# Decoder layer, one core: the FFN's weights are rounded and turned inside eleven attention rounds and kept in DRAM, and the preparation stage between the two parts is taken out

## What is computed

```python
x = x + attention(layernorm(x))                  # 16 heads of 32, causal, q k v o weights 512x512
x = x + long_conv_mixer(ctx, ctx, layernorm(x))  # head_dim 8, 32 heads, filters of length 512
x = x + ffn(layernorm(x))

def _quant_dequant(v, axis):                     # one scale for each row
    scale = jnp.maximum(jnp.max(jnp.abs(v), axis=axis, keepdims=True) / QMAX, EPS)
    return jnp.clip(jnp.round(v / scale), -QMAX, QMAX) * scale
# ffn, I = 1408
xq  = _ste(x, axis=-1);  w1q = _ste(w_gate_up, axis=-1)      # w_gate_up: 2816 x 512
gate_up = einsum('bsh,oh->bso', xq, w1q)
h   = silu(gate_up[..., :I]) * gate_up[..., I:]
hq  = _ste(h, axis=-1);  w2q = _ste(w_down, axis=-1)         # w_down: 512 x 1408
return einsum('bsi,oi->bso', hq, w2q)
```

## Time and profile before

| | us |
|---|---|
| median of 3 runs | 1321.93 |
| lowest and highest | 1319.57, 1323.46 |
| the profiled execution | 1327.34 |
| its span, first to last instruction | 1325.5 |
| from the first instruction to TensorE's last of attention | about 695 |
| preparation stage, first VectorE instruction to the mixer's first | 699.51 to 742.18 |

### The profile page before, as it was taken

The page is one execution under the profiler, slowest core; times in us unless marked ns, Lnnn a source line. Parts: engine busy times, 40 slices in busy tenths (PEclk is TensorE's granted clock), DMA queues, the critical chain, the costliest instruction groups (busy, mean ns, idle before and its releaser), DMA issues. The chain is left out here.

```text
span 1325.5 us, 33417 instructions
## 1 busy us (share of the span) xinstructions
PE 1158.6 (87%) x10082; PEld 828.7 (63%) x10082; DVE 1048.7 (79%) x3192; ACT 866.6 (65%) x1789; POOL 951.8 (72%) x1016
## 2 busy tenths in 40 slices
PE   4779998979989799899776699999999999999985
PEld 3566676757767576677543456666666666666652
DVE  5478886878868788788658688888888889888872
ACT  3467776767767677677756356666666666666664
POOL 0166675756756666667674499999999999999982
PEclk9879999998999999999886699999999999999997
DMA  5244654553445544454537244433334444444400
GB/s 193 73 152 139 199 174 159 175 174 119 142 160 174 167 135 147 145 174 154 167 134 281 90 137 120 126 124 124 131 132 130 131 132 135 135 135 135 127 25 24
DMA packets 87840, 186.57 MB, mean 141 GB/s; under 512 B 12176, under 2 KB 28816, under 8 KB 87760
## 3 DMA queue, kind: packets, MB, share of 16 engines
q1 hardware_dynamic: 86896, 185.02, 43.9%
q10 hardware_dynamic: 864, 0.66, 0.2%
HBM read 105.86 MB, written 54.61 MB: 121 GB/s over the span
## 5 line engine op out<-in xcount | busy, mean ns | idle before, releaser
L608 ACT ACTIVATE prob<-masked,negmax 128x128 f32<-128x128 f32 (+1 forms) x512 | 205.8, 452 | 129.7 <-DVE negmax L741 128.7
L741 DVE CUSTOM_DVE_ANT_0 masked<-s_ps,mask_f 128x128 f32<-128x128 f32 (+1 forms) x512 | 161.2, 352 | 43.4 <-issue 30.7
L988 PE MATMUL y_ps<-kv,toep 128*128 128x288 f16 x640 | 184.7, 289 | 1.4 <-DVE prod L1324 1.4
L990 PE MATMUL y_ps<-kv,toep 128*128 128x288 f16 x640 | 184.5, 288 | 0.0
L989 PE MATMUL y_ps<-kv,toep 128*128 128x288 f16 x640 | 184.5, 288 | 0.0
L1044 PE MATMUL f_ps<-w1T,xiT 128*128 128x512 bf16 (+1 forms) x768 | 174.7, 364 | 0.9 <-ACT xiT L1165 0.7
L1223 POOL TENSOR_TENSOR tree<-prod 128x512 f32<-128x512 f32 x128 | 163.2, 1275 | 1.2 <-DVE prod L1324 1.2
L386 POOL TENSOR_TENSOR kv_s<-kv_f,kv_s 128x1152 f16<-128x1152 f32 x64 | 154.5, 2415 | 11.4 <-ACT kv_s L622 11.3
L1172 ACT ACTIVATE silu<-gate,sx 128x512 f32<-128x512 f32 (+1 forms) x96 | 66.0, 687 | 139.6 <-DVE gate L1378 139.6
L747 DVE TENSOR_TENSOR pT_lo<-t_ps,pT_hi 128x384 f16<-128x384 f32 x256 | 140.8, 550 | 17.0 <-ACT pT_hi L616 16.5
L616 ACT CAST pT_hi<-t_ps 128x384 f16<-128x384 f32 x256 | 122.0, 477 | 41.6 <-PE t_ps L510 39.5
(11 more groups left out here) (154 smaller groups left out, 3540.3 us busy)
## 6 DMA issues: line engine op xcount, KB each, us to landing
kv_pairs<-kv_s SPq DMA_DIRECT2D x64, 576.0 KB, 4.0
kv<-kv_pairs SPq DMA_DIRECT2D x32, 1152.0 KB, 8.1
c_in<-in_ctxr SPq DMA_DIRECT2D x64, 192.0 KB, 3.5
x_in<-in_x SPq DMA_DIRECT2D x16, 512.0 KB, 6.1
q_st<-q_hi SPq DMA_DIRECT2D x128, 64.0 KB, 2.0
k_st<-k_hi SPq DMA_DIRECT2D x128, 64.0 KB, 2.0
x_res<-in_x SPq DMA_DIRECT2D x16, 512.0 KB, 5.1
x_after_attention<-x_out SPq DMA_DIRECT2D x16, 512.0 KB, 3.3
```

The source lines that it names most:

```text
L608: ins = nc.scalar.activation(prob[h % 2][:, at:at + w], masked[h % 2][:, at:at + w], ACT.Exp, bias=negmax[:, h % 2, t:t + 1], scale=-1.0)
L741: ins = nc.vector.tensor_tensor_reduce(masked[h % 2][:, at:at + w], s_ps[h % 2][:, at:at + w], mask_f[:, S - w:S], -1.0, FAR, ALU.add, ALU ...
L988: nc.tensor.matmul(dst, toep[p][:, 0, taps], c[:, 0, m], start=mt == 0, stop=False)
L990: mm = nc.tensor.matmul(dst, toep[p][:, 1, taps], c[:, 0, m], start=False, stop=mt == lt)
```

## The change

The preparation stage is gone. Its work is done in three places of attention and one of the mixer:

- Rounds 0 and 1: `w2`'s four row blocks are loaded, and VectorE takes their maxima (`w2_maxima`, steps 9 and 13 of round 0, 5 and 7 of round 1) and then the scales of the 512 rows (`w2_scales`, step 9 of round 1).
- Rounds 2 to 12, each: two row blocks of `w1` and one column block of `w2` (128 columns of all 512 rows) are loaded one round ahead (`load_w`). VectorE takes the two maxima after step 1 and the scales after step 2; ScalarE scales and rounds the two blocks after step 3 (`block_scaled`); GpSimd does the same for the columns, four instructions (`columns_scaled`). Three new jobs W turn them in fp32, in steps 5, 7 and 12, and VectorE drains each by subtracting `MAGIC` into bf16. `store_w` writes the result, 384 KB, to DRAM.
- W jobs take their turn in the same three banks, so a round has 15 jobs instead of 12. ScalarE has no part in draining them.
- After the last round's work, two transfers write the scales (2816 and 512 single fp32 elements in transposed order) to DRAM.
- The mixer loads the scales, spread over partitions by the transfer, and the turned weights (6.0 MB in SBUF in all) behind the loads of its round 0. TensorE and VectorE wait for them before its round 2. Its first loads are now issued at the mixer's own start. `w1T` has another layout, so that the gate and up matmuls read four pieces of 128 columns.
- The loop now covers rounds 2 to 11, five passes; rounds 12 to 15 are written out.

```diff
-ROUND = [("QK", 0, 1, 0, 1), ("QK", 1, 1, 2, 3), ("QK", 2, 1, 4, 5), ("QK", 3, 1, 6, 7), ("A", 0, -1, 8, 8), ("V", 0, 1, 8, 9),
-         ("A", 1, -1, 10, 10), ("V", 1, 1, 10, 11), ("X", 0, 2, 12, 12), ("X", 1, 2, 13, 13),
+ROUND = [("QK", 0, 1, 0, 1), ("QK", 1, 1, 2, 3), ("QK", 2, 1, 4, 5), ("W", 0, 0, 5, 5), ("QK", 3, 1, 6, 7), ("W", 1, 0, 7, 7),
+         ("A", 0, -1, 8, 8), ("V", 0, 1, 8, 9), ("A", 1, -1, 10, 10), ("V", 1, 1, 10, 11), ("W", 2, 0, 12, 12),
+         ("X", 0, 2, 12, 12), ("X", 1, 2, 13, 13),
          ("O", 0, -1, 13, 14), ("O", 1, -1, 14, 15)]
 G = 3
...
-LOOP0, LOOP1 = 2, B - 2
+W0, W1 = 2, 13
+LOOP0, LOOP1 = W0, W1 - 1
...
+            def load_w(i, p):
+
+                alone(sp, started)
+                if isinstance(i, int) and i < W0 + 2:
+                    sp.wait_ge(w2_max_done, DT)
+                else:
+                    sp.wait_ge(g_free, jobs_before(i - 1))
+                sp.dma_start(w_blk[p], w1[bass.ds((i - W0) * (2 * P), 2 * P)].rearrange("(t p) d -> p t d", p=P)).then_inc(blk_in[p], 16)
...
+            sp.wait_ge(w_scale_done, W1 - W0)
+            sp.dma_start(sd[0:2 * (W1 - W0)].rearrange("n p -> p n").unsqueeze(2), w_scale[:].unsqueeze(2),
+                         allow_slow_non_contiguous=True).then_inc(scales_stored, 16)
...
+                if name == "W":
+
+                    pe.wait_ge(*((blk_scaled, i - W0 + 1) if m < 2 else (col_scaled, i - W0 + 1)))
+                    for t in range(DT):
+                        src = w_blk[p][:, m, t * P:(t + 1) * P] if m < 2 else w_col[p][:, t, :]
+                        mm = nc.tensor.transpose(bank[:, t * P:(t + 1) * P], src, eye_f[:])
...
+            def block_scaled(i, p):
+
+                act.wait_ge(w_inv_done, i - W0 + 1)
+                for k in range(2):
+                    ins = nc.scalar.activation(w_blk[p][:, k, :], w_blk[p][:, k, :], ACT.Copy, bias=MAGIC, scale=w_inv[:, k:k + 1])
+                ins.then_inc(blk_scaled, 1)
...
+                    if s == 3 and has(jobs, "W"):
+                        block_scaled(i, p)
                     if s == PAIRS_HIGH[3] and not (isinstance(i, int) and i == 0):
                         pairs_high(i - 1, 3)
...
+                if name == "W":
+                    dve.wait_ge(g_full, n + 1)
+
+                    dve.wait_ge(w_stored[p], 8 * (i - p))
+                    nc.vector.tensor_scalar(w_out[p][:, m, :], bank[:], MAGIC, None, ALU.subtract).then_inc(g_free, 1)
                     return
...
+            def block_maxima(i, p):
+
+                dve.wait_ge(blk_in[p], 8 * (i - p))
+                nc.vector.tensor_reduce(w_max[:], w_blk[p], AX_X, ALU.max, apply_absolute_value=True).then_inc(w_max_done, 1)
...
+                    if s == 1 and has(jobs, "W"):
+                        block_maxima(i, p)
+                    if s == 2 and has(jobs, "W"):
+                        block_scales(i)
+                    if isinstance(i, int) and i < 2 and s in W2_MAXIMA[i]:
+                        w2_maxima(2 * i + W2_MAXIMA[i].index(s))
...
+    def load_weights(sp):
+
+        sp.dma_start(s1_b[:], sd[0:2 * IT].rearrange("n p -> (n p)").unsqueeze(0).broadcast_to([P, 2 * I_FF])).then_inc(w_loaded, 16)
+        sp.dma_start(w1T[:].rearrange("p (r n) t c -> p r (n t c)", r=IT), wd[:, :, 0:2 * D].rearrange("r p c -> p r c")).then_inc(w_loaded, 16)
+        sp.dma_start(w2T[:], wd[:, :, 2 * D:].rearrange("r p c -> p r c")).then_inc(w_loaded, 16)
...
+            first_loads(sp)
             rounds(sp, body)
...
+                if isinstance(r, int) and r == 2:
+                    pe.wait_ge(w_loaded, 64)
```

More of the change, by code:

```diff
@@ L84 @@
 JOBS_END = [("A", 0, -1, 0, 0), ("A", 1, -1, 0, 0), ("O", 0, -1, 0, 0), ("O", 1, -1, 0, 0)]
-LOOP0, LOOP1 = 2, B - 2
+W0, W1 = 2, 13
+LOOP0, LOOP1 = W0, W1 - 1
 PAIRS_HIGH = (8, 12, 15, 3)
+W2_MAXIMA, W2_SCALES = ((9, 13), (5, 7)), 9
 def round_jobs(i):
-    return [j for j in ROUND if not isinstance(i, int) or 0 <= i + j[2] < B and (i, j[0]) != (0, "V")]
+    return [j for j in ROUND if not isinstance(i, int)
+            or 0 <= i + j[2] < B and (i, j[0]) != (0, "V") and (j[0] != "W" or W0 <= i < W1)]
 def count_before(i, size):
@@ L105, in hi_before @@
 def hi_before(i):
-    return count_before(i, lambda jobs: sum(j[0] != "O" for j in jobs))
+    return count_before(i, lambda jobs: sum(j[0] not in "OW" for j in jobs))
 def first_bank(i):
@@ L233, in attention @@
     has = lambda jobs, name: any(j[0] == name for j in jobs)
-    his = lambda jobs, k: sum(j[0] != "O" for j in jobs[:k])
+    his = lambda jobs, k: sum(j[0] not in "OW" for j in jobs[:k])
     SMALLS = [(bq_raw[:], bq), (bk_s[:], bk), (mask_f[:, S - P:], mask), (bv_b[:], bv.broadcast_to([P, D])), (bo_b[:], bo.broadcast_to([P, D]))]
@@ L309, in body @@
                 first, last = isinstance(i, int) and i == 0, isinstance(i, int) and i == B - 1
+                if isinstance(i, int) and i < 2:
+                    load_w2(2 * i)
+                    load_w2(2 * i + 1)
                 if has(jobs, "X"):
@@ L317, in body @@
                     store_pairs(i - 1, 3)
+                if not isinstance(i, int) or W0 <= i + 1 < W1:
+                    load_w(i + 1, 1 - p)
                 if has(jobs, "QK"):
@@ L325, in body @@
                 store_pairs(i, 1)
+                if has(jobs, "W"):
+                    store_w(i, p)
                 if has(jobs, "O"):
@@ L371, in value_bias, with columns_scaled @@
                                         ALU.add).then_inc(attb_done, 1)
+            def columns_scaled(i, p):
+                count = 8 * (i - p)
+                if not isinstance(i, int):
+                    pool.lower_val(count)
+                pool.wait_ge(w2_inv_done, 1)
+                pool.wait_ge(col_in[p], count)
+                for n in range(DT):
+                    ins = nc.gpsimd.tensor_scalar(w_col[p][:, n, :], w_col[p][:, n, :], w2_inv[:, n:n + 1], MAGIC, ALU.mult, ALU.add)
+                ins.then_inc(col_scaled, 1)
             def pairs(i, k):
@@ L411, in body @@
                     norm(i + 2)
+                if has(jobs, "W"):
+                    columns_scaled(i, p)
                 pairs(i, 1)
@@ L822, in _, with mixer @@
                 low(B, 0, n0 + k, j, g_ps[(n0 + k) % G], h0 + his(JOBS_END, k))
[L825 removed]
+def mixer(nc, ctx, x1d, kvd, tapd, wd, sd, out, eye_f, eye_b, half_neg2, eps2):
     sb = lambda n, s, d: ctx.enter_context(nc.sbuf_tensor(n, s, d))
@@ L851, in mixer @@
     res_in = sem("res_in")
+    w_loaded = sem("w_loaded")
     st2_done, mv2_done, var2_done, rstd2_done, xq_done = (sem(n) for n in ("st2_done", "mv2_done", "var2_done", "rstd2_done", "xq_done"))
@@ L964, in body @@
                     load_res(sp, r)
+                if isinstance(r, int) and r == 0:
+                    load_weights(sp)
                 if live(r - 3, loop):
@@ L1391, in body @@
                 conv_live, ffn_live = live(r, loop), live(r - 2, loop)
+                if isinstance(r, int) and r == 2:
+                    dve.wait_ge(w_loaded, 64)
                 if conv_live:
```

225 lines of the change are left out of this document (74 added, 151 removed).

## The result

The changed kernel takes 1344.9 us (median of four runs, 1342.4 to 1348.7), the kernel before 1321.0 in the same runs: a ratio of 1.018, 95% interval 1.015 to 1.021. It is 23.9 us slower; forecast were 9.2. The profiled execution took 1345.4 us (span 1343.6), 0.5 above its median; that of before had been 5.4 above its own. Between the two profiled executions there are 18.1 us, so 5.8 of the 14.7 us between forecast and result lie in that conversion, and 8.9 in the steps.

What follows compares the result with a forecast made beforehand. It took attention rounds to be bound by VectorE's late division in step 11, then by TensorE from step 13. Terms 45.4 + 4 - 5.3 - 36.4 + 1.5 = +9.2 us, on the median, gave 1331 us, range 1311 to 1346.

Steps and rivals of the forecast that it cites:

- Rounds 2 to 12, +45.4: Attention rounds with W jobs: seven longer by 4.6 us, four behind a return by 3.3, together 45.4 us.
- Steps 1 to 5: Within a round: late maxima, ScalarE's scaling, two drains, hidden transposes, O job held by W2's drain; 4.6 us longer.
- The return, -5.3: Attention's loop: five passes instead of six, one return fewer, saving 5.3 us.
- Rounds 0 and 1, +4: First attention rounds: four maxima of 1.7 us each, three where VectorE is late; +4 us (0 to 6.7).
- The junction, -36.4: Between attention and mixer: stage removed, -42.7 us, but the convolution waits 10.5 us instead of 4.2; -36.4 us.
- the scales' store ... I take 0: Last attention round: 3328 single elements stored ahead of the last x_out; 0 us, at most 3.
- Weights for round 2, +1.5 (0 to 6): Mixer: weights arrive in time, about 27 us after its start, but kv of round 2 queues behind; +1.5 us.
- The conversion to the median: Whole kernel: the difference from the profiled execution, 1327.3 us, was added to the median, 1321.9, giving 1331.
- Rival A: Attention rounds: added work mostly hidden, 2.0 us a round, 1304 us; chance of faster 0.24, of about the same 0.17.
- Rival C: Attention rounds: TensorE's clock falls after more waits in seven rounds, +12 us, 1343; chance 0.12.
- Rival D: Mixer's round 2 weights or kv late, or scales' store holding back x_out; +6 to +10 us, 1340; chance 0.07.
- B: Attention rounds: as forecast, 3.6 to 5 us longer each, 1326 to 1337 us; chance 0.40.

Runs made afterwards that it cites:

- e5: The changed kernel with the scaling of the two w1 blocks moved from ScalarE's step 3 to GpSimd: 1337.2 us.
- e6: The changed kernel with the W2 job moved from step 12 to step 11: 1339.7 us.
- e7: The changed kernel with the w1 scaling moved to GpSimd and the W2 job moved to step 11: 1327.6 us.
- e10: The changed kernel with VectorE's block maxima over 64 of the 512 columns of each row block (scales wrong): 1344.0 us.
- e8: The kernel before with one pass of the loop and twelve rounds written out, five returns fewer: 1306.0 us.
- e4: The kernel before with one loop return fewer, five passes, rounds 12 and 13 written out: 1318.3 us.
- e14: The changed kernel with scales turned by TensorE and stored as 26 rows, and w2T and its scales loaded behind kv of round 2: 1339.2 us.
- e2: The changed kernel with w2T and its scales loaded one mixer round later, behind kv of round 2: 1341.0 us.
- e18: The changed kernel with scales turned by TensorE and stored as 26 rows, on the same chip as e17: 1341.8 us.
- e17: The changed kernel repeated unaltered, on the same chip as e18: 1349.1 us.

## Why the forecast was right in sign and too small

- **Rounds 2 to 12, +45.4 less a return of 5.3: right as a sum.** The intervals grew by 39.3 us, forecast were 40.1. With the return at some 3 us the work itself is 42, or 3.9 a round where 4.1 were forecast. Part of that is luck: some 4 us of it lie in the four returns, at 4.2 instead of 3.2 each, which no step has, and the rounds without a return do not each grow by 4.6: round 2 by 5.1, round 12 by 2.1. Steps 1 to 5 are seen in the rows: q_lo 1.8 later for ScalarE (forecast 1.95 with 0.7 for VectorE), TensorE's wait moved from step 11 to step 8 (1.69, with 0.92 left of 2.36), the O job held by W2's drain. One detail was off: the O job waits in all eleven rounds and not in seven, yet the rounds 4, 6, 8 and 10 grew by 2.6 to 3.1, not 3.3. e5, e6 and e7 tell the scaling and W2 apart; the maxima are not told by e10.
- **The return, -5.3: mis-sized.** It is 2.7 to 3.2. The price was taken against two of the shortest rounds of one execution; against all five without a return it is 81.7 - 77.3 = 4.4, and e8 has 4.0 by the traces and 3.2 by the medians.
- **Rounds 0 and 1, +4: about right.** In the two profiled executions the addition of round 2 is only 0.7 later, but that of before was a late one: it stands at 136.3 us, in e4 and e8, whose first rounds are the same, at 133.9 and 133.3. In eleven traces of versions whose first two rounds and GpSimd's work are the change's it stands at 136.6 to 140.7, median 139.0, 5.1 after the three's. That the maxima are these 5 us was not tested.
- **The junction, -36.4: the step that failed, in "the scales' store ... I take 0" and, as much, in the term for the weights behind it.** The junction shrank by 21.5 us, not by 34.9 (-36.4 + 1.5). Of the 13.4 between them 6.3 are the store's and 6.4 the weights'; in e14, with both mended, 12.5 are back. The bound, "for which I allow 3 us", came from no row; the profile had no transfer of single elements of this size to give one. The estimate that the last round leaves them time looked at the work that waits for the scales, and not at what is issued behind them on the same queue.
- **Weights for round 2, +1.5 (0 to 6): mis-sized, 7.9 measured.** The sum of bytes had all weights there 27 us after the mixer's start; w1T landed after 30.9, w2T after 33.1 and the last scales after 37.6. And it lacked that SyncE stands still when it issues behind large loads, 13.3 us for w2T and 6.4 for s2_b, with kv of round 2 behind them, for which TensorE waits last. e2's order took 4.4 of it away, and 6.4 in e14.
- **The convolution, 10.5 us after the mixer's start: right**, 11.1.
- **The conversion to the median** added 5.8 us: one execution of before, 5.4 above the median, stood for the whole. By e4 and e8 it had lost 2.4 to 3.0 us of that before round 2.
- **Rival A** fell: a round grew by 3.9 us, above the 3.3 at which it decides. **Rival C** fell as a mean: the clock was 0.98 in the ten rounds, 0.97 before. But a fall behind the new wait of V0 costs 2.3 us; of the five intervals above the profile has one with it, e17 two. **Rival D** is what came on top of B, with both of its halves and 12.7 us instead of 6 to 10; the two were not rivals, B and D could both happen, and were given no chance together.

On the store, the Trainium skill, "DMA: Bandwidth & Descriptors", in its table of rules, says to rearrange a non-contiguous last dimension; the rows of e18 and e17 agree, with the mixer's first load 3.8 and 11.4 us behind the last store. Its rate under "Bandwidth", some 10.5 ns a packet, would give the estimated 2.2 us over sixteen engines; the measured landing of 15.6 us decides.

Open is what decides whether the clock falls behind V0's wait, which is as long in the rounds without a fall, and with it whether the elements cost 1 or 7 us in the median of a kernel that is otherwise the change. Loading the weights in smaller pieces or from another engine's queue was not tried.

## What to carry to other kernels

When a stage between two parts is dissolved, cost what it covered: here its own 43 us hid the mixer's first loads (6.9 us came back) and left no weights to be loaded beside them (7.9 came back); with the scales' store, 6.3, that is 21 us. Look at every transfer for what is issued behind it on the same queue, and give a wide bound to one of a kind that no row prices. Work put into rounds of a tight chain is paid by the step that it stands ahead of, not by the engine's idle share: the same scaling cost 1.3 us a round more on ScalarE in step 3 than on GpSimd. And take the price of a rare event against the mean of the rounds without it, over more than one execution.

## What had not been expected of the hardware

From 725 to 741 us the profile counts 3767 packets, 3388 of them below 512 bytes, for 1.23 MB (77 GB/s), and the packets' times add up to 111% of sixteen engines':

```profile
DMA packets 3767, 1.23 MB, mean 77 GB/s; under 512 B 3388, under 2 KB 3388, under 8 KB 3767
...
q1 hardware_dynamic: 3767, 1.23, 111.0%
```

That is 16 engines x 16 us / 3767 = 68 ns of an engine for a packet, though most carry 4 bytes; the same engines moved 405 GB/s in the earlier trace rows. Behind loads of s1_b and w1T, SyncE took 13.3 us to issue w2T. And a fall of TensorE's clock has a price by its place: 2.3 us behind the wait in step 8 with the changed rounds, 0.2 to 1.6 behind the one in step 11 with those of before.
